# Weight preparation placed inside the first projection's units; q and k parts stored ahead of v

## The reference, cut to what matters

```python
x = x + _L0_attn_a_ref(_layernorm(x, axis=-1), ...)
x = x + _L0_ffn_ref(_layernorm(x, axis=-1), L0_ffn_w_gate, L0_ffn_w_up, L0_ffn_w_down)
x = x + _L0_attn_b_ref(_layernorm(x, axis=-1), ...)
x = x + _L0_ffn_ref(_layernorm(x, axis=-1), L0_ffn_w_gate, L0_ffn_w_up, L0_ffn_w_down)

def fp4_quant_dequant(x):          # blocks of 16 along the last dim
    scale = jnp.max(jnp.abs(xb), axis=-1, keepdims=True) / 6.0
    scale = jnp.maximum(scale, jnp.float32(1e-12))
    xn = xb / scale
    idx = jnp.searchsorted(_MID, jnp.abs(xn))
    q = _GRID[idx] * jnp.sign(xn) * scale

def _L0_attn_a_ref(x, W_qkv, b_qkv, W_o, b_o):
    qkv = x @ W_qkv.T + b_qkv
```

## Time and profile before

| What | us |
|---|---|
| Median of 3 runs (3417.87 to 3424.49) | 3421.76 |
| Profiled execution, its own time | 3419.68 |
| Its span | 3417.9 |
| VectorE, TensorE busy in 0 to 47 (weight stage) | 38.40, 8.20 |
| TensorE busy in 47 to 251 (projection A) | 183.00 of 204 |
| VectorE, TensorE busy in 1804 to 2032 (projection B) | 199.99, 186.49 of 228 |

### The profile page before, as it was taken

One profiled execution on the slowest core, in us unless ns is written; L12 is line 12 of the kernel. 1 busy time (PEld: TensorE's weight loads), 2 busy tenths in 40 slices (PEclk: granted clock), 3 DMA queues, 4 the chain that ended last, 5 costly groups with the idle time before them and its releaser, 6 DMA issues. The chain is left out here.

```text
span 3417.9 us, 92654 instructions
## 1 busy us (share of the span) xinstructions
PE 3138.9 (92%) x34732; PEld 2110.1 (62%) x34828; DVE 2614.7 (76%) x5407; ACT 1730.4 (51%) x3363; POOL 1130.2 (33%) x1888
## 2 busy tenths in 40 slices
PE   4988999999999799999997969999999979999999
PEld 2655666666666467777774535555555547777776
DVE  6548888888888589999986976556565648999997
ACT  3654667667777533333334644555555543333333
POOL 2542222222222222222224663444444432222222
PEclk9997999999999899999998989999999989999999
DMA  3764333333332122222214664544444422222221
GB/s 113 237 206 103 87 87 87 87 95 89 94 91 75 54 82 85 84 88 86 83 62 156 199 194 108 115 113 103 101 115 115 97 65 80 85 85 88 85 83 56
DMA packets 390676, 351.82 MB, mean 103 GB/s; under 512 B 111814, under 2 KB 331846, under 8 KB 390214
## 3 DMA queue, kind: packets, MB, share of 16 engines
q1 hardware_dynamic: 390342, 347.10, 37.3%
HBM read 210.12 MB, written 135.27 MB: 101 GB/s over the span
## 5 line engine op out<-in xcount | busy, mean ns | idle before, releaser
L814 DVE TENSOR_REDUCE aA_nmax<-bank 128x1 f32<-128x512 f32 (+3 forms) x1216 | 713.4, 656 | 136.3 <-PE bank L881 82.9
L853 ACT ACTIVATE aA_prob<-bank 128x512 f32<-128x512 f32 (+1 forms) x1216 | 599.0, 589 | 226.6 <-PE bank L906 224.2
L875 PE MATMUL bank<-aA_ks,aA_qs 96*32 96x512 bf16 (+14 forms) x6144 | 476.1, 324 | 42.6 <-DVE aA_nmax L814 21.9
L1219 DVE TENSOR_REDUCE aB_nmax<-bank 128x2 f32<-128x512 f32 (+1 forms) x512 | 325.1, 657 | 204.5 <-PE bank L1313 105.1
L906 PE MATMUL bank<-aA_qs,aA_ks 99*32 99x512 bf16 (+11 forms) x6144 | 460.5, 317 | 17.0 <-DMA aA_qs<-aA_rows 14.2
L1282 ACT ACTIVATE aB_prob<-bank 128x512 f32<-128x512 f32 (+1 forms) x512 | 271.5, 572 | 134.4 <-PE bank L1313 130.4
L875 PEld LDWEIGHTS bank<-aA_ks,aA_qs 96*32 96x32 bf16 x6144 | 228.0, 96 | 153.9 <-DVE aA_nmax L814 117.4
L925 PE MATMUL bank<-aA_prob,aA_vq 128*32 128x512 f32 (+3 forms) x3072 | 320.7, 489 | 0.0
L906 PEld LDWEIGHTS bank<-aA_qs,aA_ks 99*32 99x32 bf16 x6144 | 211.3, 96 | 145.0 <-issue 59.0
L797 POOL TENSOR_TENSOR aA_spare<-aA_spare 128x1 f32<-128x1 f32 x256 | 49.4, 193 | 711.2 <-ACT aA_prob L853 711.2
L1313 PE MATMUL bank<-aB_ks,aB_qs 96*128 96x256 bf16 (+3 forms) x2048 | 245.1, 258 | 38.8 <-DMA aB_own<-own_d 28.6
(11 more groups left out here) (242 smaller groups left out, 6642.2 us busy)
## 6 DMA issues: line engine op xcount, KB each, us to landing
parts_A<-pA_part SPq DMA_DIRECT2D x96, 256.0 KB, 3.3
aA_qs<-parts_A SPq DMA_DIRECT2D x192, 128.0 KB
aA_ks<-parts_A SPq DMA_DIRECT2D x192, 128.0 KB
parts_B<-pB_part SPq DMA_DIRECT2D x96, 256.0 KB, 2.6
aB_qs<-parts_B SPq DMA_DIRECT2D x192, 128.0 KB
aB_ks<-parts_B SPq DMA_DIRECT2D x192, 128.0 KB
o_A<-aA_o_sb SPq DMA_DIRECT2D x32, 512.0 KB, 3.2
o_B<-aB_o_sb SPq DMA_DIRECT2D x32, 512.0 KB, 3.1
```

What stands on the lines that cost most here:

```text
L814: nc.vector.tensor_reduce(dst, src, AX.X, ALU.max, negate=True).then_inc(s["max_taken"], 1)
L853: nc.scalar.activation(dst, src, ACT.Exp, scale=SCALE).then_inc(s["exp_done"], 1)
L875: ins = nc.tensor.matmul(out[32 * j:32 * j + 32, 0:w], qs[g][0:KROWS, h, q * P + 32 * j:q * P + 32 * j + 32], ks[g][0:KROWS, h, k0:k0 + w] ...
L1219: nc.vector.tensor_reduce(dst, src, AX.X, ALU.max, negate=True).then_inc(s["max_taken"], 1)
```

## The change

`weight_stage` is gone; a class `Weights` holds the same work in pieces, and `project_stage` of layer A calls them. SP issues x of unit 0, then four loads (identity, layer A's projection weights and its two bias tiles); every engine but SP and GpSimd waits for these four before its first step. After x of unit 1 SP issues the three weight loads and seven more. VectorE does one piece of the quantising at the end of each of its steps that normalises a unit t, for t = 1 to 15: a scale (three instructions) at t = 1, 3, 7, and one pass over a weight at each of the others, the last multiply of all three weights now on VectorE. ScalarE does its three absolute values at the ends of steps t = 3, 7, 11. The absolute values and the sums share one tile each for the three weights. After the last step TensorE turns the weights, four (gate, up) or two (down) transposes to a group, 14 groups through two banks; ScalarE copies a group at once, and VectorE makes the bias rows. In both layers SP stores the six parts of a unit ahead of its v.

```diff
--- before.py
+++ after.py
-def weight_stage(nc, core, bank, const_loads, w_gate, w_up, w_down, ident, wgT, wuT, wdT, bo_sb, brow, pick):
...
+class Weights:
+    def __init__(self, nc, core, mem, bank, first_loads, later_loads, w_gate, w_up, w_down, ident, wgT, wuT, wdT,
+                 bo_sb, brow, pick):
...
+        mag, sum_ = sb("wm", [P, 8 * D]), sb("ws", [P, 8 * D])
+        self.mag, self.sum = ({k: x[0:rows[k], 0:cols[k]] for k in "gud"} for x in (mag, sum_))
...
+        self.turns = []
+        for k, out in (("g", wgT), ("u", wuT)):
+            for c in range(DC):
+                for i in (0, 4):
+                    self.turns.append((k, [j * D + c * P for j in range(i, i + 4)], P,
+                                       out[:, c, i * WROWS:(i + 4) * WROWS]))
+        for c, (c0, cw) in enumerate(F_CHUNKS):
+            self.turns.append(("d", [i * F + c0 for i in range(2)], cw, wdT[0:cw, c, :]))
+    def load_first(self, sp):
+        for dst, src in self.first_loads:
+            sp.dma_start(dst, src).then_inc(self.first, 16)
+    def load_later(self, sp):
+        for k, src, parts in self.sources:
+            sp.dma_start(self.w[k][:, :].rearrange("p (a k) -> p a k", a=parts),
+                         src.rearrange("(a p) k -> p a k", p=self.rows[k])).then_inc(self.loaded[k], 16)
+        for dst, src in self.later_loads:
+            sp.dma_start(dst, src).then_inc(self.consts, 16)
+    def wait_first(self, eng):
+        eng.wait_ge(self.first, 16 * len(self.first_loads))
+    def wait_later(self, eng):
+        eng.wait_ge(self.consts, 16 * len(self.later_loads))
...
+    def on_vector(self, dve, t):
+        nc = self.nc
+        if t in (1, 3, 7):
+            k = {1: "g", 3: "u", 7: "d"}[t]
+            dve.wait_ge(self.loaded[k], 16)
+            nc.vector.tensor_reduce(self.amax[k][:, :], blocks(self.w[k][:, :]), AX.X, ALU.max,
+                                    apply_absolute_value=True).then_inc(self.steps[k], 1)
+            dve.wait_ge(self.steps[k], 1)
+            nc.vector.tensor_scalar(self.s22[k][:, :], self.amax[k][:, :], UP / 6.0, 1e-12 * UP, ALU.mult,
+                                    ALU.max).then_inc(self.steps[k], 1)
+            dve.wait_ge(self.steps[k], 2)
+            nc.vector.reciprocal(self.rinv[k][:, :], self.s22[k][:, :]).then_inc(self.steps[k], 1)
+        if t in (2, 4, 8):
+            k = {2: "g", 4: "u", 8: "d"}[t]
+            dve.wait_ge(self.steps[k], 3)
+            nc.vector.scalar_tensor_tensor(blocks(self.v2[k][:, :]), blocks(self.w[k][:, :]), TIE_DOWN,
+                                           spread(self.rinv[k][:, :]), ALU.mult, ALU.mult).then_inc(self.steps[k], 1)
+        if t in (5, 9, 12):
+            k = {5: "g", 9: "u", 12: "d"}[t]
+            dve.wait_ge(self.mag_made, "gud".index(k) + 1)
+            nc.vector.scalar_tensor_tensor(self.sum[k], self.mag[k], 1.0, self.v2[k][:, :], ALU.max,
+                                           ALU.add).then_inc(self.steps[k], 1)
+        if t in (6, 10, 13):
+            k = {6: "g", 10: "u", 13: "d"}[t]
+            dve.wait_ge(self.steps[k], 5)
+            nc.vector.scalar_tensor_tensor(self.v2[k][:, :], self.mag[k], 1.0, self.sum[k], ALU.max,
+                                           ALU.subtract, reverse1=True).then_inc(self.steps[k], 1)
+        if t in (11, 14, 15):
+            k = {11: "g", 14: "u", 15: "d"}[t]
+            dve.wait_ge(self.steps[k], 6)
+            nc.vector.tensor_tensor(blocks(self.w[k][:, :]), blocks(self.v2[k][:, :]), spread(self.s22[k][:, :]),
+                                    ALU.mult).then_inc(self.quantised[k], 1)
...
+    def on_scalar(self, act, t):
+        if t in (3, 7, 11):
+            i = (3, 7, 11).index(t)
+            k = "gud"[i]
+            act.wait_ge(self.steps[k], 4)
+            if i:
+                act.wait_ge(self.steps["gud"[i - 1]], 6)
+            self.nc.scalar.activation(self.mag[k], self.v2[k][:, :], ACT.Abs, scale=UP).then_inc(self.mag_made, 1)
+    def turn(self, pe):
+        for i, (k, starts, cw, _) in enumerate(self.turns):
+            pe.wait_ge(self.quantised[k], 1)
+            if i >= 2:
+                pe.wait_ge(self.copied, i - 1)
+            r = self.rows[k]
+            for j, c0 in enumerate(starts):
+                ins = self.nc.tensor.transpose(self.bank[0:cw, i % 2, j * r:(j + 1) * r], self.w[k][:, c0:c0 + cw],
+                                               self.ident[0:r, 0:r])
+            ins.then_inc(self.turned, 1)
+    def copy_turned(self, act):
+        for i, (k, starts, cw, dst) in enumerate(self.turns):
+            act.wait_ge(self.turned, i + 1)
+            self.nc.scalar.activation(dst, self.bank[0:cw, i % 2, 0:len(starts) * self.rows[k]],
+                                      ACT.Copy).then_inc(self.copied, 1)
...
@@ -329,15 +342,21 @@
                         need(sp, s["xn_ready"], k.t - 1)
                         sp.dma_start(xin[k.p][:, :, :], x_v[k.t]).then_inc(x_loaded[k.p], 16)
+                        if extra and k.t == 0:
+                            extra.load_first(sp)
+                        if extra and k.t == 1:
+                            extra.load_later(sp)
                     if (k := at(STORE)):
-                        sp.wait_ge(s["v_ready"], k.t + 1)
-                        sp.dma_start(v_v[k.t // 2, k.t % 2], vs[k.p][:, :, :, :]).then_inc(v_stored[k.p], 16)
                         for q in range(2):
                             for j in range(3):
                                 sp.wait_ge(s[f"part{j}_ready"], k.t * NCH + 2 * q + 2)
                                 sp.dma_start(parts_v[j, k.t, q],
                                              part[j][k.p][:, 2 * q:2 * q + 2, :]).then_inc(part_stored[j][k.p], 16)
+                        sp.wait_ge(s["v_ready"], k.t + 1)
+                        sp.dma_start(v_v[k.t // 2, k.t % 2], vs[k.p][:, :, :, :]).then_inc(v_stored[k.p], 16)
                 in_line(NU, STORE, step)
+                if extra:
+                    extra.wait_later(sp)
                 for q in range(2):
                     sp.wait_ge(v_stored[q], 16 * (NU // 2))
                     for j in range(3):
@@ -347,6 +366,8 @@
             def _(pool):
                 nc.gpsimd.memset(half[:, :], -0.5).then_inc(s["const_ready"], 1)
                 pool.wait_ge(s["const_ready"], 1)
+                if extra:
+                    extra.clear_rows(pool)
                 def last_part(c, i):
@@ -451,6 +472,8 @@
                         if c:
                             for i in range(1, NCH):
                                 cut(c, i)
+                        if extra and k:
+                            extra.on_vector(dve, k.t)
                         return
                     if k:
                         stats(k)
@@ -470,7 +493,11 @@
                         odd(m, 1)
                 if rope:
                     dve.wait_ge(s["tab_loaded"], 16)
+                if extra:
+                    extra.wait_first(dve)
                 in_line(NU, STORE, step)
+                if extra:
+                    extra.bias_rows(dve)
             @block.scalar
             def _(act):
@@ -537,7 +564,13 @@
                         next_part(c, 2)
                     if c:
                         next_part(c, 3)
+                    if extra and k:
+                        extra.on_scalar(act, k.t)
+                if extra:
+                    extra.wait_first(act)
                 in_line(NU, STORE, step)
+                if extra:
+                    extra.copy_turned(act)
             @block.tensor
             def _(pe):
@@ -570,7 +603,11 @@
                                 ins = nc.tensor.matmul(ps_v[:, a, :], xT[m.p][:, c, a, :], w_sb[:, c, 2 * D:3 * D],
                                                        start=(c == 0), stop=(c == DC - 1))
                         ins.then_inc(s["v_done"], 1)
+                if extra:
+                    extra.wait_first(pe)
                 in_line(NU, STORE, step)
+                if extra:
+                    extra.turn(pe)
 def max_units():
@@ -1779,22 +1816,22 @@
         b_v, b_col = core.sb("b_v", [P, D]), core.sb("b_col", [P, 4])
         wgT, wuT = core.sb("wgT", [P, DC, F]), core.sb("wuT", [P, DC, F])
         wdT = core.sb("wdT", [P, len(F_CHUNKS), D])
-        loads = [(ident[:, :], ident_d), (ident_b[:, :], identb_d),
-                 (mask_sb[:, :], mask_d),
-                 (b_v[:, :], A_b[2 * D:3 * D].partition_broadcast(P)),
-                 (b_col[:, :], A_bcol)]
-        for i, (w, wo, bo) in enumerate(((A_w, A_wo, A_bo), (B_w, B_wo, B_bo))):
-            loads += [(w_sb[i][:, :, :], w.rearrange("(c p) n -> p c n", p=P)),
-                      (wo_sb[i][:, :, :], wo.rearrange("(c p) n -> p c n", p=P)),
+        first = [(ident[:, :], ident_d), (w_sb[0][:, :, :], A_w.rearrange("(c p) n -> p c n", p=P)),
```

(68 more changed lines are left out.)

103 lines of the change are left out of this document (4 added, 99 removed).

## The result

The changed kernel takes 3392.45 us (median of 4 runs, 3390.68 to 3395.4) against 3421.66 for the kernel before, run beside it (4 runs, 3417.87 to 3424.49): 0.9915 of the time, 95% interval 0.9902 to 0.9927. That is 29.2 us less, where 32.0 were forecast. The profiled execution took 3392.58, its span is 3390.8, 27.1 under the span of before.

A forecast was written before the change was run, and what follows sets the result against it. Start taken as latency with TensorE nearly unused, the projection's steady state as bound by TensorE. Start -41.1, pieces +9.0, turns -0.9, B's stores +1.0 sum to -32.0; from 3420.8, rounded, 3389.0, range 3379 to 3401.

The forecast's parts named there:

- The start: Ahead of the first projection: removing the weight stage brings unit 1's q and k from 74.65 to 33.5, -41.1 us.
- T0: VectorE's start in the first projection, after the first x load and four more loads: taken as 9.5 us.
- the chain of 8.5 from statistics to TensorE: First projection's start: from unit 2's statistics through cuts, normalisation and xT copy to TensorE's unit 1, 8.52 us.
- the two 88-partition weights (1.44 MB) at 208 GB/s take 6.9 us: Loads queued ahead of unit 2's x: with the rest at 348 GB/s, that x is there at 24.5.
- Rival 4: First projection: waits let TensorE's clock fall to 1.2 GHz, about 11 us more per unit, 3543; chance 0.03.
- The pieces: Weight work at VectorE's step ends in projection A: delays the next bias addition, +9.0 us together (1 to 13).
- The lock: VectorE and GpSimd's shared SBUF port pair: whoever starts second fully blocks; a kernel without it some 8 us better.
- Rival 1: Projection A: GpSimd's part is out of the way, only scale pieces cost, 1 us: 3380.8; chance 0.16.
- rival 3: Projection A: weight pieces hide nowhere, 34.4 us on the path, -6.7 in all: 3414; chance 0.04.
- The turns and A's stores: Projection A's end: turns to 250.0, next stage 250.5 against 251.38, -0.9; stores end some 4.7 earlier, covered by turns.
- B's stores: Projection B's end: v stored last, issued 0.6 later and a longer transfer taken at 0.4, +1.0 us (0.5 to 1.6).
- Rival 2: Heavier start: x2 or x3 behind 5.8 MB comes at 28, pieces cost 13, -22.4 in all: 3398.4; chance 0.15.

## Why the prediction was right or wrong

- **The start: wrong by 4.1.** -37.05 instead of -41.1, outside the -42.6 to -38 given. T0 and the chain of 8.5 from statistics to TensorE held. The step that failed is "the two 88-partition weights (1.44 MB) at 208 GB/s take 6.9 us". The 208 came from a stretch of mixed transfers. In the run with loads in shares the gate weights travel alone at 12 to 14 us:

```profile
12.00:14.00 2.00, 0.00 (x0) 0.00 (x0) 1.79 (x10) 1.88 (x3) 0.09 (x1) 1.00 0.66 143
```

  143 GB/s at a DMA share of 0.66. By then unit 1's x has gone ahead of them and nothing follows until 15.51. At that rate the two take 10.1, and x2 would be there at 27.7 of the 29.09 measured. The changed kernel's own stretches fit that:

```profile
10.00:12.00 2.00, 0.00 (x0) 0.00 (x0) 0.77 (x7) 0.00 (x0) 1.01 (x1) 1.00 0.81 165
...
18.00:20.00 2.00, 1.20 (x2) 0.68 (x3) 1.93 (x3) 0.75 (x1) 0.00 (x0) 1.00 1.09 225
20.00:22.00 2.00, 2.00 (x4) 0.83 (x3) 0.37 (x1) 0.00 (x0) 0.00 (x0) 1.00 1.07 321
```

  From 10 to 20 its transfers, the two weights with later loads beside them, run at 165 to 225 GB/s. Only from 20 on do they reach 321 to 349, where the sum had 348 for all but 6.9 us. The prediction's own upper bound, "all of it up to the fourth megabyte at the slower rate would give 28", is the case that came. The last 1.4 us are not a gap left by SP's late issue, for the DMA share is never under 0.81 between 4 and 26. Of the 6.36 MB, 6.24 had moved by 26, yet x2 landed at 29.07, 10.2 after its issue, where the sum allowed 0.5 for landing. Unit 3's x, issued at 19.37, was under way beside it; whether that is the reason was not tried. The Trainium skill ("DMA: Bandwidth & Descriptors", on why a DMA increments its semaphore by 16) says that a transfer is spread over the largest number of engines up to 16 that divides the outermost dimension of both its source and its destination. For 88 partitions that would be 11, 0.69 of 16, and the row's 0.66 is near it.
- **The clock: not in the sum.** "Were the start warm, x2 would still govern" was right for the start of unit 1, but I priced the wait for x2 only as lateness. By it TensorE stands idle for 5.7 us, and the unit behind runs its first passes at 1.2 GHz: 2.6 us over a unit (13.77 - 11.19), in place of the 0.8 forecast for piece 2, which lay under it. Net it is 1.2, for piece 3 hid under it in part. The size is not fixed: in the run with v stored first, whose unit 1 has the same piece, unit 2 began 13.00 after unit 1, and in the run without pieces, where the clock fell too, 12.88. Rival 4 had named "one slow x load per unit" as enough. Here it was one load in all; between units 2 and 15 the clock held, so the rival itself did not come.
- **The pieces: right.** The lock was real, passes of 3.20, 0.79 us per long one (0.8 forecast), 0.12 per short one (0.15), the down scale 0.82 (0.95). Piece 15, taken at 0, cost 0.11. From unit 2's start on they cost 7.3 of a forecast 8.2, and what is missing is piece 3, the up scale: 0.47 for 1.2. Its rows in the timeline of the changed kernel:

```profile
49.68 1.01 ACT L562 ACTIVATE pA_xT<-bank 128x1024 f32<-128x1024 f32 x1
...
49.97 2.27 DVE L212 TENSOR_REDUCE wa_u<-w_u 88x128 f32<-88x2048 f32 x1
...
53.44 1.16 DVE L456 TENSOR_TENSOR pA_vs<-bank,b_v 128x1024 f32<-128x1024 f32 x1
```

  The copy ends at 50.69, and the bias addition starts 2.70 after the 50.74 at which TensorE could have gone on, 2.74 in the forecast. But TensorE, late from its slow unit 1, started only at 51.37, and 0.63 of the piece was covered. Rival 1 falls with the 3.20, rival 3 with the 11.98.
- **The turns and A's stores: right.** 8.1 us of turns (7.9), the tail 1.04 shorter (0.9). The stores' gain, 4.3, is real where nothing covers it (4.7 forecast), and is covered by the turns as forecast.
- **B's stores: right in kind, mis-sized.** +1.9 instead of +1.0. The issue is the 0.66 as forecast; the term that failed is the longer transfer, taken at 0.4: v is written 3.56 after its issue against 2.39 for a part, 1.17.
- **The sum.** From unit 1's first pass to the mark the changed kernel takes 177.06 (37.60 to 214.66), the one before 167.23 (74.86 to 242.09; the forecast's 74.65 is the weight load ahead of that pass): +9.83, of which 2.6 is the clock's unit and 7.3 the pieces. -37.26 + 9.83 - 1.04 = -28.5 for the start to attention A, against -33.0; B +1.9. The unchanged stages gave -0.4 between them in the profiled executions, -3.6 of attention A against +3.2 elsewhere. So -27.1 in span and -29.2 in the medians, and the forecast of 3389.0 lies 3.5 under the measured 3392.45. The two changed stages miss by 5.4 (4.5 and 0.9); that the total misses by less is luck, the variation of whole executions and not the sum. Rival 2 (3398.4) had the right cause and nearly the time, x2 behind 5.8 MB at 28, with too high a price for all the rest.

## What to carry to other kernels

When work is taken out of a start, price what the first unit then waits for by the bytes and issues queued ahead of it, and give each load the rate of its own shape, not that of a mixed stretch; the wait costs again if it is long enough for TensorE's clock to fall. Ask of every hole where VectorE can take a piece what GpSimd does at that moment, and put the piece into a wait of VectorE's, not between the last cut and the work that the next unit waits for: here that was worth 7.5 us (214.66 to 207.11) for moving a few lines. A saving at a stage's end counts only as far as nothing else ends there.

## What was not expected of the hardware

- An issue on SP's queue can hold SP itself: 5.36 us for one load of 128x1408, with about 3.5 MB issued ahead of it; the same load took 0.51 when each load went out alone.
- A load into 88 partitions moved at 143 GB/s, the loads into 128 partitions at 20 to 26 of the changed kernel at 321 to 349, its stores at 42 to 44 at 383.
- The stretches from 16 to 26 of the changed kernel show a clock of 1.00, yet unit 0's 16 passes, from 18.80 on, take 8.76, against 7.03 later. The trace holds no record of the clock before 22.12, so the 1.00 up to there is no reading. What a first unit costs is read from its duration.
- The span of an unchanged stage of 930 us differs by up to 5.9 us between executions of kernels that differ only elsewhere, which is of the size of the gains studied here; the marks of stages repeated within 0.7.
